# Three buffers for gathered rows, with the direct gathers issued two strips ahead

## What is computed

```python
Wh = layernorm(x) @ W                       # 8192 x 256
e = leaky(Wh @ a1 [:, None] + Wh @ a2 [None, :], 0.2)
e = where(adj > 0, e, -9e15)
x = x + elu(softmax(e, axis=1) @ Wh)
y = layernorm(x); i = argmax(y @ router_w.T + router_b)
h = relu(y @ W1[i] + b1[i])
x = x + relu(h @ W2[i] + b2[i])
```

## Time and profile before

| what | us |
|---|---|
| median of 3 runs | 1158.03 |
| lowest, highest | 1155.84, 1163.48 |
| the profiled execution | 1156.93 |
| its span, first to last instruction | 1155.2 |

### The profile page before, as it was taken

One profiled execution on the slowest core, in us unless ns is written; L12 is line 12 of the kernel. 1 busy time (PEld: TensorE's weight loads), 2 busy tenths in 40 slices (PEclk: granted clock), 3 DMA queues, 4 the chain that ended last, 5 costly groups with the idle time before them and its releaser, 6 DMA issues.

```text
span 1155.2 us, 24922 instructions
## 1 busy us (share of the span) xinstructions
PE 898.1 (78%) x4394; PEld 568.0 (49%) x4395; DVE 869.5 (75%) x4264; ACT 794.4 (69%) x1339; POOL 655.8 (57%) x702
## 2 busy tenths in 40 slices
PE   5898387877887888887788888877788866378995
PEld 4676244444544444544444544444454545256774
DVE  6786287877887888888788888878788866645663
ACT  3667487886887877888687878877778811046663
POOL 4785455664655566655556656555655546236664
PEclk9999598998999999999899999989989976679998
DMA  9997798997999999999899999989989993045551
GB/s 346 395 367 282 295 376 339 375 375 287 395 356 349 353 383 363 382 355 362 318 380 363 375 355 366 363 329 374 368 332 368 306 230 106 21 127 161 169 170 56
DMA packets 84778, 357.32 MB, mean 309 GB/s; under 512 B 26070, under 2 KB 52655, under 8 KB 68353
## 3 DMA queue, kind: packets, MB, share of 16 engines
q1 hardware_dynamic: 56226, 296.78, 69.4%
q0 software_dynamic: 27776, 60.06, 15.2%
q10 hardware_dynamic: 736, 0.05, 0.0%
HBM read 343.67 MB, written 32.05 MB: 325 GB/s over the span
## 4 chain that ended last, share of the span: by engine, by line
DVE 26%; DMA 23%; issue 21%; PE 18%; POOL 8%; DVEq 2%; POOLq 0%; ACT 0%; ACTq 0%
DMA G_all<-wh_table,idx 12%; DMA regions<-x,posu 8%; POOL G_all L613 6%; PE psW L1501 5%; PE psO L1711 3%; DVE top_word L880 2%; PE psO L1585 2%; DMA out_x<-raw_all,tok 1%; DVE xn L1157 1%; POOL out_x L675 1%; PE psF L1519 1%; DVE begun L1057 1%; POOL regions L635 1%; DVE lidx L1172 1%; DVE oh L1180 1%
## 5 line engine op out<-in xcount | busy, mean ns | idle before, releaser
L613 POOL DMA_INDIRECT G_all<-wh_table,idx x384 | 397.7, 1036 | 134.6 <-issue 124.8
L722 ACT ACTIVATE sg<-raw_all,minus_tiny 128x1024 fp8e4<-128x1024 int32 x256 | 311.5, 1217 | 0.2
L725 ACT ACTIVATE sg<-raw_all,minus_half 128x1024 fp8e4<-128x1024 int32 x256 | 311.1, 1215 | 0.0
L1510 PE MATMUL psO<-word_no,share 128*128 128x512 bf16 x885 | 244.4, 411 | 0.0
L635 POOL DMA_INDIRECT regions<-x,posu x64 | 67.2, 1051 | 213.1 <-DVE idx L1049 117.0
L1585 PE MATMUL psO<-G_all,diag 128*128 128x256 f32 x640 | 163.5, 405 | 22.0 <-DVE diag L1114 22.0
L1585 PEld LDWEIGHTS psO<-G_all,diag 128*128 128x128 f32 x640 | 124.9, 202 | 63.7 <-issue 46.9
L1519 PE MATMUL psF<-sg,fold_w 128*128 128x512 bf16 x512 | 138.7, 395 | 7.6 <-DVE top_word L880 2.8
L1510 PEld LDWEIGHTS psO<-word_no,share 128*128 128x128 bf16 x885 | 93.7, 111 | 92.9 <-issue 26.8
L755 ACT ACTIVATE pr<-ee,nmx 128x16 f32<-128x16 f32 x64 | 19.7, 307 | 154.9 <-DVE nmx L1105 154.9
L675 POOL DMA_INDIRECT out_x<-raw_all,tok x81 | 79.2, 978 | 57.9 <-issue 30.6
(11 more groups left out here) (221 smaller groups left out, 1853.2 us busy)
## 6 DMA issues: line engine op xcount, KB each, us to landing
raw_all<-in_adj SPq DMA_DIRECT2D x128, 2048.0 KB, 10.0
raw_all<-regions SPq DMA_DIRECT2D x84, 130.0 KB, 2.1
wh_table<-G_all POOLq DMA_DIRECT2D x16, 520.0 KB, 9.0
x_sb<-in_x SPq DMA_DIRECT2D x8, 1024.0 KB, 18.4
G_all<-wh_table,idx POOLq DMA_INDIRECT x384
regions<-pad_row SPq DMA_DIRECT2D x32, 130.0 KB
x_sb<-in_L_ffn_W SPq DMA_DIRECT2D x4, 512.0 KB
x_sb<-in_L_ffn_W SPq DMA_DIRECT2D x8, 256.0 KB
```

The source lines that it names most:

```text
L613: pool.indirect_dma_start(out=G[par][:, k, :], out_offset=None, in_=table[:, :], in_offset=bass.IndirectOffsetOnAxis(ap=idx[par][:, k:k + ...
L722: act.activation(sign_of[par][q][0], raw_of[b][q % 2][0], ACT.Identity, bias=minus_tiny[:, 0:1], scale=TINY, saturate=False)
L725: act.activation(sign_of[par][q][1], raw_of[b][q % 2][1], ACT.Sign, bias=minus_half[:, 0:1], saturate=False).then_inc(a_sg, 1)
L1510: pe.matmul(psO[par][:, :], share[:, :], word_no[:, 0:2, :].rearrange("p q w -> p (q w)"), start=True, stop=True)
```

## The change

The gathered rows, x1, posu and their semaphores get three buffers, chosen by the strip modulo 3. The direct gathers of strip u+2 are issued in step u, where those of strip u+1 were; the gather by slot of strip u+1 comes ahead of them. On VectorE `indices(u + 2)` now stands behind `slot_scores(u)`, where `indices(u + 1)` stood at the head of the step. For the third buffer the loop of VectorE, TensorE and GpSimd becomes one of 9 turns of six steps in place of 27 turns of two.

```diff
-        G_all = sb("G_all", [P, 2 * GROUP, ROW])
-        G = [G_all[:, i * GROUP:i * GROUP + GATHERS, :] for i in range(2)]
+        G_all = sb("G_all", [P, THIRDS * GATHERS, ROW])
+        G = [G_all[:, i * GATHERS:(i + 1) * GATHERS, :] for i in range(THIRDS)]
...
-        x1 = [sb(f"x1{i}", [P, ROW]) for i in range(2)]
+        x1 = [sb(f"x1{i}", [P, ROW]) for i in range(THIRDS)]
...
             def loop(u0, u1):
-                if u1 > u0:
-                    with eng.Fori(u0 // 2, u1 // 2) as i:
-                        for par in range(2):
-                            step(i * 2 + par, par, does(u0))
+                assert u0 % 2 == 0 and (u1 - u0) % 6 == 0
+                with eng.Fori(0, (u1 - u0) // 6) as i:
+                    for c in range(6):
+                        turn, rest = divmod(u0 + c, THIRDS)
+                        step(i * 6 + (u0 + c), c % 2, (i * 2 + turn, rest), does(u0))
...
-            def step(u, par, do):
+            gather_edges(0, 0, 0)
+            gather_tail(0, 0, 0)
+            gather_edges(1, 1, 1)
+
+            def step(u, par, slot, do):
 
                 if do.fetch:
-                    gather_waits(u + 1, 1 - par)
-                    gather(1 - par, 0, KD, gat)
-                    gather_tail(u + 1, 1 - par)
+                    gather_tail(u + 1, 1 - par, third(slot, 1)[1])
+                if do.prepare:
+                    gather_edges(u + 2, par, third(slot, 2)[1])
                 if do.post:
-                    inverse_std(u - 1, 1 - par)
+                    inverse_std(u - 1, third(slot, -1)[1])
                 if do.place:
-                    scatter(u - 2, par)
+                    scatter(u - 2, third(slot, -2)[1])
...
-            v.memset(G_all[:, :, D + 2:ROW], 0.0)
+            v.memset(G_all[:, 0:2 * GROUP, D + 2:ROW], 0.0)
+            v.memset(G_all[:, 2 * GROUP:THIRDS * GATHERS, :], 0.0)
...
                 if do.fetch:
-                    indices(u + 1, 1 - par)
                     rows_of_slots(u + 1, 1 - par)
                 if do.attend:
-                    slot_scores(u, par, half_up(u, par) * GATHERS)
+                    slot_scores(u, par, slot)
+                if do.prepare:
+                    indices(u + 2, par)
+                if do.attend:
                     penalties(u)
...
                 if do.post:
-                    post_x1(w, 1 - par, x_rows(w), None if isinstance(w, int) and w < 2 else half_done(w, 1 - par))
+                    post_x1(w, buf, x_rows(w), None if isinstance(w, int) and w < THIRDS else reused * 16)
```

More of the change, by code:

```diff
@@ L190, in gat_moe @@
         posf = sb("posf", [P, 1])
-        posu = [sb(f"posu{i}", [P, 1], u32) for i in range(2)]
+        posu = [sb(f"posu{i}", [P, 1], u32) for i in range(THIRDS)]
         nbi = sb("nbi", [P, E], i32)
@@ L274, in gat_moe @@
         pe_slot_p = sem("pe_slot_p")
-        gat = [sem(f"gat{i}") for i in range(2)]
+        gat = [sem(f"gat{i}") for i in range(THIRDS)]
         null_out = sem("null_out")
@@ L290, in gat_moe @@
         xr_in = [sem(f"xr_in{i}") for i in range(2)]
-        sc_out = [sem(f"sc_out{i}") for i in range(2)]
+        sc_out = [sem(f"sc_out{i}") for i in range(THIRDS)]
         v_flag = sem("v_flag")
@@ L329, in does, with third, strips_of_third @@
                         post=1 <= u < NS + 1, place=2 <= u < NS + 2)
+        def third(slot, d):
+            turn, rest = slot
+            return turn + (rest + d) // THIRDS, (rest + d) % THIRDS
+        def strips_of_third(k):
+            return (NS + THIRDS - 1 - k) // THIRDS
         def rounds(eng, step):
@@ L492, in _ @@
                 sp.wait_ge(v_plan, 2 * PLAN_STEPS)
[L494 to L497, removed]
+                for par in range(2):
+                    sp.wait_ge(sc_out[par], 16 * strips_of_third(par) + 8 * NS)
+                    sp.nop(nofuse=True)
             sp.wait_ge(v_plan, PLAN_STEPS)
@@ L504, in _ @@
             sp.nop(nofuse=True)
[L505 to L508, removed]
+            for k in range(THIRDS):
+                sp.wait_ge(sc_out[k], 16 * strips_of_third(k))
+                sp.nop(nofuse=True)
             def load_block(b, r, turn):
@@ L861, in _ @@
             v.memset(mean_sb[:, :], 0.0)
+            for k in range(THIRDS):
+                v.memset(x1[k][:, :], 0.0)
             for par in range(2):
-                v.memset(x1[par][:, :], 0.0)
                 v.memset(w1_b[par][:, :], 0.0)
@@ L1079, in rows_of_slots, with slot_scores @@
                 v.tensor_scalar(idx[par][:, KD:KD + 1], slot_key[:, :], -1.0, float(N), ALU.mult, ALU.add).then_inc(v_tail_idx, 1)
-            def slot_scores(u, par, i16):
-                v.wait_ge(gat[par], i16)
+            def slot_scores(u, par, slot):
+                turn, buf = slot
+                v.wait_ge(gat[buf], turn * (16 * GATHERS) + 16 * GATHERS)
                 v.wait_ge(pe_row_s, u)
-                v.tensor_scalar(slot_s[:, :], slot_col[par][:, :], G[par][:, KD, D:D + 1], None, ALU.mult).then_inc(v_slot_s, 1)
+                v.tensor_scalar(slot_s[:, :], slot_col[par][:, :], G[buf][:, KD, D:D + 1], None, ALU.mult).then_inc(v_slot_s, 1)
             def penalties(u):
@@ L1191, in place_pick, with place_position @@
                                        op0=ALU.mult, op1=ALU.add, accum_out=posf[:, :]).then_inc(v_place, 1)
-            def place_position(w, par):
+            def place_position(w, buf):
                 v.wait_ge(v_place, w * VE + VE + 8)
-                v.scalar_tensor_tensor(out=posu[par][:, :], in0=posf[:, :], scalar=-1.0, in1=posf[:, :],
+                v.scalar_tensor_tensor(out=posu[buf][:, :], in0=posf[:, :], scalar=-1.0, in1=posf[:, :],
                                        op0=ALU.mult, op1=ALU.max).then_inc(v_place, 1)
@@ L1199, in _ @@
             indices(0, 0)
+            indices(1, 1)
             rows_of_slots(0, 0)
@@ L1243, in half_done, with step @@
                 return (w - par) * 8
-            def step(u, par, do):
+            def step(u, par, slot, do):
                 t, w, y = u + LAG, u - 1, u - 2
+                reused, buf = third(slot, -1)
                 if do.fetch:
-                    indices(u + 1, 1 - par)
                     rows_of_slots(u + 1, 1 - par)
                 if do.attend:
-                    slot_scores(u, par, half_up(u, par) * GATHERS)
+                    slot_scores(u, par, slot)
+                if do.prepare:
+                    indices(u + 2, par)
+                if do.attend:
                     penalties(u)
@@ L1260, in step @@
                 if do.attend:
-                    softmax(u, par)
+                    softmax(u, slot[1])
                 if do.decode:
@@ L1308, in step @@
                     place_pick(y)
-                    place_position(y, par)
+                    place_position(y, third(slot, -2)[1])
                 if isinstance(u, int) and u == NS - 1:
@@ L1640, in step @@
                 if do.attend:
-                    weighted_sum(u, par)
+                    weighted_sum(u, par, slot[1])
                 if do.place:
```

61 lines of the change are left out of this document (30 added, 31 removed).

## The result

| | before | changed |
|---|---|---|
| median of 20 runs each, same chips, us | 1152.66 | 1161.48 |
| lowest, highest | 1140.93, 1163.48 | 1158.04, 1169.4 |
| span of the profiled execution | 1155.2 | 1160.5 |

What follows compares the result with a forecast made beforehand. VectorE's own sequence, broken by two waits for DMA, was taken as the bound, with the DMA engines nearly as full. 1156.9 - 63.2 (gathers, scatter) - 12.5 + 38.4 + 5 = 1124.6, said as 1125 us; range 1100 to 1150 us.

Steps and rivals of the forecast that it cites:

- What bounds the kernel: In the 66 steps of stretch 2, VectorE's own sequence sets the pace, broken by two waits for DMA.
- The gathers: VectorE's `slot_s` waits for gathered rows go, except the first strip's, as the gather by slot leaves 6.8 us earlier: 38.2 us off.
- The scatter: With three buffers `x` waits for a scatter one step older, so its whole wait goes: 25.0 us off.
- The old branches: VectorE's waits of 0.47 us behind the loop's branch, for 27 turns, go: 12.5 us off.
- The new branches: VectorE's 8 branches back fetch code that isn't there, at 4.8 us each, between 2.99 and 6.6: 38.4 us on.
- Rival (c): Slower: each branch back costs two fetches one after the other, 9.6 us, giving 1168 us; chance 0.10.
- The DMA engines: In stretch 2 they just fit, but a stalled VectorE stops ScalarE, which frees the buffers: 5 us on.
- (a): Code stays or its fetch is hidden; branches cost 4 us and the DMA engines bind: 1117 or 1102 us; chance 0.25.
- (b): DMA is the bound already; VectorE's waits go to ScalarE waiting for `raw_all`, time stays 1150 to 1157 us; chance 0.10.
- (d): Gathers are still late as landing grows with load; half of the 38.2 us stays, 1144 us; chance 0.07.
- One sign that the prediction named: ScalarE waiting for `raw_all`, with a DMA share of 0.98 and more, would show the DMA bound.

Runs made afterwards that it cites:

- the run with short loads: The changed kernel with the adjacency loads of the steps cut to an eighth of their columns: 1230.54 us (one run).
- The written-out kernels: The changed kernel and the kernel before, each with VectorE's 66 steps written out without a loop: 1185.9 us (0.9538 of before) and 1212.24 us (0.9772).
- the kernel written out: The changed kernel with the steps of VectorE, TensorE and GpSimd all written out: 1097.79 us, 0.9557 of the kernel before.

## Why the prediction was wrong

**What bounds the kernel: right.** VectorE's sequence with the two waits for DMA did set the pace. When they went, nothing else took their place but the branch: outside the turns' ends the steps are at 12.5 us, and `lg` and `xn` wait 6.7 us together from 180 to 940 us.

**The gathers, 38.2 us off: right in the trace.** 54.5 - 19.6 = 34.9 us went over the span, 3.3 less than forecast: 1.5 us were left in the steps, and the first strip's wait is 18.0 us in place of 16.3. The argument that the gather by slot leaves 6.8 us earlier and so beats any wait of up to 4.2 us held; its undoing cost 23 us on the other kind of chip, where other engines are later as well.

**The scatter, 25.0 us off: right in the trace, not shown by a run.** The row is gone. On the chips where the wait was put back it cost nothing. There TensorE was late behind it. Whether it is worth its 25 us on the first kind was not measured alone, but the account of the loop closes to within 3 us with its 18.9 us in it.

**The old branches, 12.5 us off: a little more, 15.1.** There were 26 of them, not 27 (the 27th entry of the earlier trace rows is the 0.20 us at the loop's entry), and a step with a branch was 0.58 us longer, not 0.47.

**The new branches, 38.4 us on: this is the step that failed.** That the code isn't held was right, with 68 more packets in place of the 5 or 6 a turn, some 44, that were named. At some 63 bytes an instruction, as the written-out code has it (30 more packets for 52 more steps of 75 recorded instructions), 696 of them are 5.4 packets. So some 3 a turn bring code that the turn doesn't execute; one packet starts between 1.0 us ahead of the branch and 1.4 us behind it, too early to be the awaited one. The price was wrong. It was bounded by 6.6 us, as one fetch of 2.99 us and up to 3.6 us of load, and the middle of 2.99 and 6.6 was taken. The first stop alone is 5.7 to 7.0 us, 6.4 in the mean (51.0 / 8). So the 6.6 us, a fetch with the typical load on it, was about the value and not the upper end, as every branch falls where the DMA share is 0.97 or more; taking the middle gave away 8 x 1.6 = 13 us. Behind it comes a second stop of some 2 us, which the bounds did not hold at all (16 us). And the turns show 0.6 us more (5 us), about the 4.5 us that VectorE waits for `lg` from TensorE in five of them. Together 9.0 us, 72.3 us in place of 38.4. Rival (c) named this: two fetches one after the other, 9.6 us, and a point of decision at 8.8 us a branch. It was argued down with the earlier trace rows, where the sequencer runs on without a second stop. But there the DMA share is 0.19 (1013 to 1017 us), and in the run with short loads the second stop shrinks in the same way to the 0.39 us that are there without a branch too. The row was read for a loaded stretch from a quiet one.

**The DMA engines, 5 us on.** No wait of ScalarE for the adjacency appeared in the changed kernel, so this term is not seen as such; its share is 0.92. What was not in the sum is the pace, 0.06 us a step or some 3 us. Its cause is open. It may be that the loads bunch behind each stop, or the counts computed from the loop counter, of which a six-step loop has other forms; neither was tried by itself.

**The sum by its terms.** It forecast -63.2 - 12.5 + 38.4 + 5 = -32.3 us, and the profiled span grew by 5.3, so 37.6 us were missed. The branches are 33.9 of them. The gathers gained 3.3 less, the rest of the loop's account is 6.0 (5.5, and 0.5 of new waits beside the 1.5 of `slot_s`), and the parts outside the loop became 13.9 us shorter where 15.9 us of waits of `slot_s` and `x` went, 2.0 more. On the other side the old branches gave 2.6 more, and the 5 us for the DMA engines were not needed. 33.9 + 3.3 + 6.0 + 2.0 - 2.6 - 5 = 37.6. At the 38.4 us forecast for the branches the change would have been 28.6 us or 2.5% faster. The written-out kernels, in which neither has a branch, differ by 26 us on the other kind of chip.

**The other rivals.** (a) held neither in its condition nor its time, but its bound did: 1102 to 1117 us was the time with the branches gone, and the kernel written out, where they are gone, took 0.9557 of the time before, which is 1106 of its 1157, at a DMA share of 0.99. (b) fell: the late gathers were not a sign of full DMA engines in the kernel before, since they went although the share ahead of each branch is 0.97 or more. (d) fell: 1.5 us of waits were left in the stretch. One sign that the prediction named is wrong: full DMA engines would show as ScalarE waiting for `raw_all`. In the written-out kernel they show as gathers landing late.

## What to carry to other kernels

A third buffer that needs a loop of three or six steps costs a longer body, and once the body of an engine is no longer held each branch back is a fetch by DMA, here 9 us on the engine that sets the pace; look at the packets on the instruction queues, and keep the body at the size that shows no refetch, or write the steps out, which here beat every loop. A price that is seen where an engine or queue is quiet is the lower bound for a loaded stretch (here 2.99 us quiet, 6.4 us loaded); where every occurrence falls into the loaded stretch, take the upper bound, which here was still too low by the stop that only the load brings out. Take off a wait in full only where nothing is late next behind it: the same 11 us of `x` were worth nothing on a chip where `lg` was later.

## What the runs showed of the hardware

- A loop body of 236 recorded VectorE instructions was held, 467 and 696 were not (28, 103 and 96 packets of 8 KB in the run). TensorE's six-step body showed no refetch (14 packets of 16 KB against 12).
- A branch back to code that isn't held took 2.9 us at a DMA share of 0.29, and 6.4 us and a second stop of about 2 us at 0.92 in the mean and 0.97 or more ahead of the branch. The packet that ends the first stop starts 1.0 to 1.3 us behind the branch in the run with short loads and 3.7 to 5.2 us behind it in the changed kernel. At the branch of 256.61 us it lasts 0.32 us, and VectorE goes on 1.65 us behind its end. So what the load adds is time before the packet.
- With all three engines written out, VectorE had no wait for issue at those places, with 36 (16 KB) and 63 (8 KB) packets in the whole run, and an undisturbed step took 11.92 us against 12.43 in a held loop. What in the loop costs the 0.5 us was not tried apart; the 60 recorded instructions of VectorE's sequencer a step against 17 are one candidate (some 41 of the 60 are ALU_OP and FUSED_REGOPS, which the written-out steps don't show).
- The same program took 1148 us on one chip and 1244 to 1247 on others. A single difference in us from one chip is no price for another.
